# The projection whole ahead of the messages on TensorE, and gates ahead of copies on ScalarE, in a two-layer graph kernel

## The reference

```python
def reference(x, adj, nodemask, ...):
    # layer 0: gated convolution; with adj in {0, 1} only relation 1, the loop direction, has edges
    h = x @ W_loop.T;  g = h @ Wg_loop.T
    vals = (h + b_loop) * sigmoid(g + bg_loop)
    x = layernorm(x + relu(adj.T @ vals))
    # layer 1: one relation is met
    x = layernorm(x + (mask @ x) @ weight[0] + bias)
    return x
```

## Time and profile before

| | us |
|---|---|
| median of 3 runs | 158.79 |
| lowest and highest | 158.68, 159.75 |
| the profiled execution | 159.41 |
| its span, first to last instruction | 157.7 |
| TensorE busy in the span | 148.8 (94%) |
| GpSimd, VectorE, ScalarE busy | 125.7, 124.1, 122.8 (80%, 79%, 78%) |

### The profile page before, as it was taken

How to read it: one execution, slowest core, us unless ns; L and a number is a source line. 1 busy time by engine, 2 the same in 40 slices (tenths; PEclk the granted TensorE clock), 3 DMA queues, 4 the chain that set the end, 5 groups by cost and what they waited for, 6 DMA issues and landing times.

```text
span 157.7 us, 3520 instructions
## 1 busy us (share of the span) xinstructions
PE 148.8 (94%) x1040; PEld 136.7 (87%) x1040; DVE 124.1 (79%) x325; ACT 122.8 (78%) x255; POOL 125.7 (80%) x195
## 2 busy tenths in 40 slices
PE   7999999999999999999999999999999999999910
PEld 3688999999999999999999999999999999999800
DVE  1359988888988888887988888887888878989980
ACT  3357876979797997979797997979797997769850
POOL 0606698797979799797979799797979799797970
PEclk9999999999999999999999999999999999999995
DMA  4899999989797988979797989989693929211053
GB/s 126 292 405 394 370 389 404 390 265 389 198 382 230 331 303 258 354 241 398 177 392 209 356 290 286 340 237 373 192 393 130 381 92 303 86 69 69 4 201 138
DMA packets 19606, 42.73 MB, mean 271 GB/s; under 512 B 2177, under 2 KB 3073, under 8 KB 19585
## 3 DMA queue, kind: packets, MB, share of 16 engines
q1 hardware_dynamic: 14544, 25.76, 48.6%
q0 software_dynamic: 4752, 16.52, 30.3%
q10 hardware_dynamic: 288, 0.20, 0.4%
HBM read 34.08 MB, written 8.39 MB: 269 GB/s over the span
## 4 chain that ended last, share of the span: by engine, by line
POOL 65%; PE 15%; issue 13%; DVE 1%; POOLq 1%; ACT 0%; DVEq 0%
POOL rstd L339 31%; POOL x L353 26%; PE hg_ps L423 7%; POOL adj_sb L326 4%; POOL adjt_sb L333 3%; PE loop_ps L439 2%; PE msg_ps L458 2%; PE msg_ps L413 1%; PE y_ps L497 1%; PE hg_ps L407 1%; POOL rstd L363 1%; POOLq L59 1%; DVE s_sb L808 0%; ACT gate L607 0%; POOLq L234 0%
## 5 line engine op out<-in xcount | busy, mean ns | idle before, releaser
L339 POOL TENSOR_TENSOR rstd<-var,power 128x8 f32<-128x8 f32 (+1 forms) x36 | 53.8, 1496 | 18.5 <-DVE var L787 18.4
L423 PE MATMUL hg_ps<-w_all,xt_sb 128*128 128x256 f32 x256 | 65.7, 382 | 0.0
L353 POOL TENSOR_SCALAR x<-s_sb,mean_neg,rstd 128x128 f32<-128x128 f32 x120 | 52.2, 448 | 3.4
L423 PEld LDWEIGHTS hg_ps<-w_all,xt_sb 128*128 128x128 f32 x256 | 44.6, 193 | 4.1 <-issue 0.3
L626 ACT ACTIVATE out_sb<-z_sb,rstd 128x128 f32<-128x128 f32 x120 | 38.1, 390 | 0.4 <-POOL rstd L339 0.4
L800 DVE TENSOR_TENSOR vals<-hg_ps,gate 128x512 f32<-128x512 f32 x32 | 22.1, 690 | 19.3 <-ACT gate L607 19.3
L439 PEld LDWEIGHTS loop_ps<-vals,adj_sb 128*128 128x128 f32 x256 | 33.3, 191 | 1.9 <-issue 0.2
L598 ACT ACTIVATE hg_ps<-gate_b 128x1024 f32<-128x1024 f32 (+1 forms) x32 | 31.8, 998 | 3.2 <-DVE vals L800 2.6
L458 PEld LDWEIGHTS msg_ps<-adjt_sb,x 128*128 128x128 f32 x248 | 31.4, 191 | 3.1 <-issue 1.5
L439 PE MATMUL loop_ps<-vals,adj_sb 128*128 128x128 f32 x256 | 33.8, 275 | 0.1
L458 PE MATMUL msg_ps<-adjt_sb,x 128*128 128x128 f32 x248 | 33.2, 277 | 0.0
(11 more groups left out here) (64 smaller groups left out, 48.2 us busy)
## 6 DMA issues: line engine op xcount, KB each, us to landing
xt_sb<-x_t_dram SPq DMA_DIRECT2D x32, 256.0 KB, 4.9
x_sb<-x_dram SPq DMA_DIRECT2D x32, 256.0 KB, 4.2
out<-out_sb SPq DMA_DIRECT2D x31, 256.0 KB, 4.7
adj_sb<-adj_dram POOLq DMA_DIRECT2D x15, 512.0 KB, 5.2
adjt_sb<-adj_t_dram POOLq DMA_DIRECT2D x15, 512.0 KB, 6.5
adjt_sb<-adj_t_dram POOLq DMA_DIRECT2D x2, 256.0 KB, 6.7
first_edges<-adj_dram SPq DMA_DIRECT2D x1, 256.0 KB, 4.2
adj_sb<-adj_dram POOLq DMA_DIRECT2D x1, 256.0 KB, 6.3
```

The lines of the kernel that those rows point to most:

```text
L339: nc.gpsimd.tensor_tensor(rstd[:, c % RSTD_RING, first:end, :].rearrange("p l b -> p (l b)"), var[:, c % 2, first:end, :].rearrange("p l b ...
L353: done = nc.gpsimd.tensor_scalar(x1[:, q % X1_RING, batch(b)], s_sb[:, q % S_RING, batch(b)], mean_neg[:, c % 2, b:b + 1], rstd[:, c % RST ...
L423: last = nc.tensor.matmul(hg_ps[:, q % 2, b, :], xt_sb[:, q % XT_RING, batch(b)], w_gate, start=False, stop=True, skip_group_check=True)
```

## The change

TensorE's slot has the projection whole, and the messages behind it. ScalarE does the gates of a slot ahead of the copy of its messages. The small changes: three warm-up matmuls in place of five at line 413; `mean_neg` is gone, and GpSimd and VectorE subtract the mean where it stands in the statistics (with a wait in `first_stats` that guards the ring of statistics); the second norm of group 30 runs on ScalarE, behind that of group 29, and ScalarE issues its store.

```diff
+        def mean_of(c, b):
+            return stats[:, c % STATS_RING, b // 2, 3 * (b % 2) + 1:3 * (b % 2) + 2]
...
-            sp.wait_ge(out_dve, 1)
-            store(LAST - 1)
             for p in range(2):
                 span = slice(2 * p * P, 2 * (p + 1) * P)
-                sp.wait_ge(out_dve, p + 2)
+                sp.wait_ge(out_dve, p + 1)
...
                         x1[:, q % X1_RING, batch(b)], s_sb[:, q % S_RING, batch(b)],
-                        mean_neg[:, c % 2, b:b + 1], rstd[:, c % RSTD_RING, 0, b:b + 1], ALU.add, ALU.mult)
+                        mean_of(c, b), rstd[:, c % RSTD_RING, 0, b:b + 1], ALU.subtract, ALU.mult)
...
-            for _ in range(5):
+            for _ in range(3):
                 nc.tensor.matmul(msg_ps[:, :], warm[:, :], warm_wide, start=True, stop=True)
...
-                else:
-                    messages(t - MSG_LAG)
                 project(t, (2, 3))
-                if t == MSG_LAG:
-                    messages(0)
+                messages(t - MSG_LAG)
                 loop_sum(t - LOOP_LAG)
                 message_weights(t - Y_LAG)
...
+                gates(t)
                 copy_messages(t - MSG_LAG)
-                gates(t)
...
             norm2(GROUPS - 3, every)
+            norm2(GROUPS - 2, every)
+            act.wait_ge(out_done, GROUPS - 1)
+            act.dma_start(out[GROUPS - 2], out_sb[:, (GROUPS - 2) % OUT_RING, :])\
+                .then_inc(out_st[(GROUPS - 2) % OUT_RING], 16)
...
-                if first == 0:
-                    await_count(dve, x1_done, c - 2)
-                    ts(mean_neg[:, c % 2, :], both[:, 0:GB, 1], -1.0, None, ALU.mult)
...
             def first_stats(q):
                 dve.wait_ge(s_done, q + 1)
+
+                await_count(dve, x1_done, q - STATS_RING + 1)
...
-            last_norm2(LAST - 1, 0, GB, root_count(GROUPS + 2, 1))
             last_norm2(LAST, 0, 2, root_count(GROUPS + 3, 1))
             last_norm2(LAST, 2, GB, root_count(GROUPS + 3, 2))
```

More of the change, by code:

```diff
@@ L89, in build @@
         var = sb("var", [P, 2, 2, GB], F32)
-        mean_neg = sb("mean_neg", [P, 2, GB], F32)
         nmr = sb("nmr", [P, 2, GB], F32)
@@ L792, in offsets @@
                 dve.wait_ge(root_done, root_count(c, 0))
-                tt(nmr[:, list(ON_ACT).index(q), :], mean_neg[:, c % 2, :], rstd[:, c % RSTD_RING, 0, :], ALU.mult)\
+                means = stats[:, c % STATS_RING, 0:2, :].rearrange("p c (i k) -> p (c i) k", k=3)[:, :, 1]
+                stt(nmr[:, list(ON_ACT).index(q), :], means, -1.0, rstd[:, c % RSTD_RING, 0, :], ALU.mult, ALU.mult)\
                     .then_inc(nmr_done, 1)
```

## The result

The changed kernel takes **189.61 us** (median of 4 runs, 188.88 to 191.98), the kernel before 159.27 in the same runs: 1.188 times as long, interval 1.182 to 1.195. The forecast was 160.2. The profiled execution of the changed kernel (191.98 us) is the longest of its four; its first loads came late, and its first loop sum starts 2.1 us later than in the trace of before (11.83 against 9.73 us).

A forecast was written before the change was run, and what follows sets the result against it. It took TensorE, issuing without a hole, to bound the loop. Terms of 3.12 - 0.34 - 0.16 - 0.3 - 0.9 made +1.4 us on the median of 158.79, so 160.2 us; range 158.4 to 161.8.

The forecast's parts named there:

- mean_neg: GpSimd's first norm subtracting the mean: hidden even at a tenth more per pass, 0; VectorE's removed instructions -0.16 us.
- the three: Rivals: wait for the copy hidden, 157.1 us, 0.10; ScalarE late every second slot, 164.1, 0.04; clock level rising later, 163.2, 0.06.
- TensorE's slot: Loop on TensorE: message weights wait for ScalarE's copy, 0.12 us in 26 slots, +3.1; messages never wait for x1, -0.34.
- The sum of the loop: Loop on TensorE: loss of 3.12 us at the message weights less 0.34 us from messages no longer waiting.
- ScalarE's order: ScalarE in the loop: gates and copy change places in time, the copy is not delayed, margin 0.07 us; cost 0.
- The waits for x1: TensorE ahead of the messages: messages moved back 0.87 us never find x1 late; about six places of 0.06, -0.34 us.
- The gain of 0.16: VectorE ahead of the first roots and in the last groups: 32 removed instructions, 0.08 us for each place, -0.16.
- The start: Three warm-up matmuls: projection starts 0.58 to 0.85 us earlier, clock level rises at the same instant; -0.3 us (-0.85 to 0).
- The rival of the late clock: Start on TensorE: idle before the first tile keeps the clock level low through both first projections; 163.2 us, chance 0.06.
- The end: Last groups: group 30's norm leaves VectorE, GpSimd's last power shortens, last store issued one us earlier; -0.9 us (-1.2 to -0.3).

The follow-up runs named there:

- second run with forms: Kernel before with GpSimd's four first-norm passes in four operation forms, one per graph, none subtracting: 167.46 us against 159.43.

## Why the prediction was wrong, point by point

**The step that failed** is the one on *mean_neg*: "no row shows a subtraction there, the nearest is its addition in the same pass", and then "even a tenth more per pass stays hidden: 0". The operation was unknown and its cost was bounded by a guess, a tenth, where no row gave an upper end. It is 0.347 us a pass more (795 against 448), 77%. Four passes make 1.39 us a slot. The cover named there was 0.12 to 0.85 us per slot, so the cover was gone by a wide margin: two powers (1.69 + 1.66), eight passes (3.13 + 3.12) and two issues of loads (0.63 + 0.54) are 10.77 us of the 10.89 that two slots now take (they overlap by some hundredths, so the view has 10.67 busy). The term is not 0 but some +29 us, by the run with the subtraction alone.

No rival had it either: the three were about TensorE's order, ScalarE and the clock. The time is outside the range because the range took its ends from the terms that were thought about, and the one taken for nothing had none.

The cover was also less than it looked. GpSimd's idle time was 0.12 us in a slot with loads and 0.85 in one without, 0.48 on average; but 0.11 of it stands behind each power and stays even where GpSimd sets the pace, so 0.01 and 0.74 could be used, 0.37 on average. Even the guess, a tenth of four passes, is 0.18 us, more than a slot with loads had. The second run with forms asks for 0.45 us more per slot. That is 0.08 over the mean, and it costs 0.31 a slot (8.0 us over 26): in its trace GpSimd waits for VectorE's variances in the slots without loads, and is late in those with loads.

```profile
85.81 1.67 POOL L339 TENSOR_TENSOR rstd<-var,power 128x8 f32<-128x8 f32 x1 [0.30 <-DVE var L794]
```

What is spare in one slot doesn't carry into the next in full.

**TensorE's slot: right, and measured.** 0.12 us per slot were forecast from a single row of slot 3; in the run with the order alone they stand in the slots of the loop, and the parts are the same 0.20, 0.60 and 0.11. The sum of the loop, 3.12 - 0.34 = +2.8, was measured at +3.1 (2.7 to 3.5). In the changed kernel this loss lies mostly under GpSimd's: 188.4 with the subtraction alone, 189.6 with all. The reading that TensorE issues without a hole, and that any wait of its own is paid once a slot, is what made this step right; that GpSimd ran close behind it was in the same rows, was said there, and got no price.

**ScalarE's order: right.** With and without the exchange the slot is 4.52 to 4.53 us.

**The waits for x1: right in the traces.** Moved back by 0.43 us, six of seven vanish, and the six slots that were 0.06 us longer no longer are. (6 x 0.06 is 0.36 and not 0.34.) By time the gain is 0.4 with an interval that reaches zero. The gain of 0.16 put down to the removed instructions was not measured by itself.

**The start: the size came out, by luck.** -0.3 forecast, -0.4 measured with an interval that holds zero, and with the two long executions nothing is left of it. The account was that the level rises at the same instant as before. In the trace of that run the 16 projections went on for 3.69 us, so nearly all ran at the upper level from 5.41 on: the rise came sooner, and the first loop sum 0.80 us earlier than in the trace of before (8.93 against 9.73). But the trace of before is one execution. Here are its five warm-up matmuls of line 413, and then those of the run with the subtraction alone, which leaves them as they are (ns, least, median and most):

```profile
L413 PE MATMUL msg_ps<-warm x5: 634/634/634, 3.7 to 5.4; 128*128 128x512 bf16 x5
```
```profile
L413 PE MATMUL msg_ps<-warm x5: 379/380/634, 3.7 to 4.8; 128*128 128x512 bf16 x5
```

Nine traces have these five matmuls. In the four where all of them take 634 ns the first loop sum starts at 9.73 to 9.97 us, in the five where some are shorter, so that the level rose sooner, at 8.83 to 9.15. So the rise near 6.7 us, from which the -0.3 was worked out, held for one execution. The Trainium skill (TensorE: Matmul & The Clock Gate, part 1) lets the rise come at different points from run to run. These traces agree, and one trace with three matmuls can't tell what the edit did to it. The rival of the late clock showed itself once, in the profiled execution of the changed kernel:

```profile
6.49 5.50 PE L423 MATMUL hg_ps<-w_all,xt_sb 128*128 128x256 f32 x16 [1.29 <-DVE hg_ps L752]
```

There the gate bias landed 4.2 us after its issue instead of 2.6, TensorE was idle for 1.29 us, and the 16 projections took 5.50 us. That is the cost that this rival named, in kind and not in full size, with a late load beside the two missing matmuls; which of them set it off isn't shown.

**The end: right mechanism, half the size.** -0.9 forecast, -0.4 (-0.8 to -0.1) measured. The power was 0.27 us shorter, as worked out (0.81 instead of 1.08). What was over-sized is the store: issued 1 us earlier, as forecast, it took 0.36 us longer to issue and 0.2 to 0.8 longer to land, with ScalarE's store issued 0.3 us ahead of it (153.60). That three stores close together are the reason is likely and was not tried. The interval contains the least gain given, -0.3.

## What to carry to other kernels

An operation that the trace doesn't hold has no price, however alike it looks to one that it holds: give it an end that is a multiple, and look for whom it would make the bound. Where the bound engine is full, the next ones matter as much: list each engine's spare time per slot, slot by slot and not as a mean, take off the idle time that stays when that engine sets the pace, and price every changed instruction against the smallest. On the same grounds one row can be enough for the other side: a stretch of the old trace that already holds the new order told the loss per slot to a hundredth of a us. A reading of the start from one trace, though, is a reading of one execution: see several before a term is built on it.

## What the runs showed of the hardware

On GpSimd the time of a pass over 128x128 depends on which operations it does, from 448 to 810 ns with two numbers for each partition and from 371 with a constant in place of one, while VectorE's two passes of the same norm in the early groups take 0.66 us with the addition and with the subtraction (before, then after):

```profile
14.38 0.66 DVE L823 TENSOR_SCALAR x<-s_sb,mean_neg,rstd 128x128 f32<-128x128 f32 x2
16.41 0.66 DVE L824 TENSOR_SCALAR x<-s_sb,stats,rstd 128x128 f32<-128x128 f32 x2
```

The Trainium skill (GPSIMD Engine Reference, 3.1 Elementwise) says that GpSimd does an elementwise operation in a software loop where VectorE has a datapath. A cost that goes by the pair of operations on GpSimd alone fits that and doesn't prove it, and the one operation that the page has a measured time for, an addition of two tensors, would not have told the forms apart. A constant in place of a number for each partition saved about 75 ns in two pairs (448 to 371, 795 to 722). Why one operation alone is slower than a multiplication with an addition was not tried.
